# Second attention layer of a four-layer graph kernel: where the output bias and the second beta are added

## Chip, cores and metric

The kernel runs on one core of a Trainium2 chip. The metric is the device time of one execution in microseconds (us). Everything is float32. The engines are named as the profile names them: PE is the matrix engine (PEld its weight loads), DVE the vector engine, ACT the scalar engine, POOL GpSimd, SP the queue that issues plain DMAs.

## What is computed

A node table x of 50,000 rows of 128 goes through four layers; each is `x = layernorm(x + layer(x))`. Layers 0 and 1 are graph attention and graph convolution, layers 2 and 3 are edge attention over 25,000 edges sorted by target node. The change is in layer 2:

```python
q, k, v = x @ Wq + bq, x @ Wk + bk, x @ Wv + bv           # 8 heads of 16
score = einsum('ehd,ehd->eh', q[dst], k[src]) / sqrt(16) + edge_attr @ We + be
attn = softmax of score over the edges of each dst
out = segment_sum(attn * v[src], dst)
h = out @ Wo + bo + x                                      # bo: the output bias
x3 = layernorm(x + layernorm(h) * gamma + beta)            # beta: the "second beta", beta2 in the kernel
```

## The kernel before

Rows that no edge reaches are computed first, in a long phase over the whole node table. What follows is done for edges only, in slots of 128 edges. The last two phases are the edge attentions, `kind == 2` (layer 2) and `kind == 3` (layer 3), each one loop over 49 iterations L of 512 edges (`G_CH`, `CH = 512`, `SUB = 4` slots of 128).

Each phase is a software pipeline written as steps. A plan (lines 1679 to 1687 for layer 2) gives every step a place; the step of iteration L stands at `place + 138 * L` (`HOP4_LAG = 138`), and `Line.run` (line 860) sorts the steps of each engine by that number. So each engine does its steps of different iterations in a fixed order, and waits in that order: an engine whose next step isn't ready waits, and all behind it wait too. One turn of the loop does one step of each kind; the steps of late places belong to older iterations. Buffers form a ring of five (`RING = 5`), so that what is written for L reuses the buffer of L - 5.

The steps around the change, in layer 2:

- `gather` (POOL, lines 1776 to 1780, helper line 895): eight indirect DMAs, four that fetch the source rows `gs` and four that fetch the target rows `own`. It waits until the previous users of the buffers, five iterations ago, are done.
- `residual` (POOL, lines 1766 to 1774): two additions of 128x512, `xo = own + bo` and `w = own + beta2`.
- `turn_x`, `products`, `values`, `scores` (PE): `turn_x` turns `gs`, `own` and the edge attributes; `products` are the key and query products (lines 1835 and 1836), `values` the value product (1848), `scores` two accumulated products (1856 and 1858) whose result is waited for by DVE.
- `maximum` (DVE, lines 931 to 938): starts with a copy (931), then a running maximum (933) and three element-wise operations (935, 936, 938); `sums` (DVE, 953, 957, 960) makes messages and running sums `den` and `num`.
- `turn_sums` (PE): turns `num` (line 368, `ps<-ident,num`), multiplies columns for the next layer's query (1883), and turns `den` into rows (965). `divide` (DVE, 2023, 973, 975, 978) follows it.
- `turn_o` (PE) turns the divided result `o` (in the buffer `kb`), `copy_oT` (ACT, 1940) copies it out of PSUM into `xsT`, `turn_q` (PE) turns the finished rows of an older iteration (`msg`), and `rows_o` (PE, lines 1867 to 1871) multiplies by Wo: four blocks of 128 columns (helper `rows_times`, lines 371 to 378, where the product is line 374), each opening its own part of the PSUM bank K[7].
- `h_res` (DVE, lines 2034 to 2039) adds the bank K[7] and `xo`. Two layernorms (`ln_vector`, lines 319 to 332) with `x3_pre` (2043 to 2050, which reads `w`) between them follow.

Within one turn of the loop DVE's order is: scale of an older iteration (329, 332), `maximum`, `h_res`, statistics (319), `x3_pre` (2047, 2050), statistics, `sums`, scale, `qk` (2006), `divide`. PE's order is: `turn_o`, `turn_q`, `rows_o`, `turn_x`, `products`, `values`, `turn_sums`, `scores`.

An earlier phase has already a product of the kind that the change adds, in `xw_rows` (line 1303): a 1x128 row of ones times a 1x512 bias row opens a bank (line 1306), and four 128x128 blocks are accumulated on it (line 1308).

Of the kernel before, what the change touches and what calls it, by code (L numbers as in the profile page):

```python
# [15 lines left out]
F32 = mybir.dt.float32  # L16
# [3 lines left out]
ALU = mybir.AluOpType  # L20
# [3 lines left out]
P = 128  # L24
D = 128
SUB = 4
CH = P * SUB
NODES, EDGES = 50000, 25000
RING = 5
# [18 lines left out]
def build(nc, x, src, dst, ea32, ea64, ew, w, out):  # L48
# [13 lines left out]
    def S(name):  # L62
        if name not in sems:
            if len(sems) == len(handles):
                handles.append(ctx.enter_context(nc.semaphore(f"signal_{len(handles)}")))
            sems[name] = handles[len(sems)]
        return sems[name]
# [32 lines left out]
    ones = sb("ones", [1, P])  # L100
# [11 lines left out]
    Wq, Wk, Wv, Wo = (sb(n, [P, D]) for n in ("Wq", "Wk", "Wv", "Wo"))  # L112
    bq, bk, bv = (sb(n, [P, 1]) for n in ("bq", "bk", "bv"))
    bo, gamma2, beta2 = (sb(n, [P, D]) for n in ("bo", "gamma2", "beta2"))
# [16 lines left out]
    def rows4(t):  # L131

        return t.rearrange("p (j f) -> p j f", j=SUB)

    def each_row(row):
        return row[:, None, :].to_broadcast([P, SUB, D])
# [234 lines left out]
    def rows_times(pe, to, tT, W, bias_row=None):  # L371

        for j in range(SUB):
            last = nc.tensor.matmul(to[:, j * D:(j + 1) * D], tT[:, j * P:(j + 1) * P], W[:],  # L374
                                    start=True, stop=bias_row is None)
            if bias_row is not None:
                last = nc.tensor.matmul(to[:, j * D:(j + 1) * D], ones[:], bias_row[:], start=False, stop=True)
        return last
# [22 lines left out]
    with ExitStack() as tmp:  # L401
# [4 lines left out]
        xsT, xdT = ring("xsT", 2, (P, CH)), ring("xdT", 2, (P, CH))  # L406
# [574 lines left out]
    K = [ps[:, k, :] for k in range(8)]  # L981
# [9 lines left out]
    with ExitStack() as tmp:  # L991
# [9 lines left out]
        own = tile("own")  # L1001
# [672 lines left out]
    for kind in (2, 3):  # L1674
# [2 lines left out]
        table, ea = tables[kind + 1], (ea32 if kind == 2 else ea64)  # L1677
        if kind == 2:
            lag, plan = HOP4_LAG, {
                "load": (1, "ea_in pen_in"), "residual": (30, "xo x2b"),  # L1680
                "turn_x": (38, "xsT_ps xdT_ps eaT_ps"), "copy_xT": (66, "xsT xdT eaT"), "products": (84, "k_ps q_ps"),
                "values": (101, "v_ps"), "copy_z": (112, "kb"), "qk": (120, "qk"), "scores": (129, "z_ps"),
                "maximum": (149, "M_first M dz Dm0 Dm"), "gather": (-420, ""), "exps": (181, "p F"),
                "sums": (232, "msg den num"), "turn_sums": (255, "num_rows"), "divide": (270, "dn rd divided"),
                "turn_o": (285, "oT_ps"), "copy_oT": (296, "oT"), "rows_o": (304, "wo_ps"), "h_res": (317, "h_res"),
                **ln_plan("d", 326, 394, 419, 439), "x3_pre": (478, "dg x3_pre"), **ln_plan("e", 494, 510, 528, 547),
                "store": (565, "stored"), "turn_q": (574, "x3T_ps"), "copy_q": (592, "x3T")}
        else:
            lag, plan = HOP5_LAG, {
                "load": (1, "ea_in pen_in ew_in q_in own_in"),  # L1690
                "turn_x": (72, "xsT_ps eaT_ps"), "copy_xT": (100, "xsT eaT"), "residual": (105, "xo"), "products": (136, "z_ps"),
                "gather": (-420, ""), "values": (163, "v_ps"), "copy_z": (174, "kb"), "qk": (218, "zl"),
                "maximum": (227, "M_first M dz Dm0 Dm"), "exps": (261, "p F"), "sums": (286, "msg den num"),
                "turn_sums": (342, "num_rows"), "divide": (403, "dn rd divided"), "x4_pre": (416, "x4_pre"),
                **ln_plan("f", 474, 490, 516, 522), "scatter": (540, "")}
        new_phase()
        with ExitStack() as tmp:
            hop = Line(tmp, f"t{kind}", plan, lag, "xsT pen kb qk p F den num msg xo " + ("xdT w" if kind == 2 else "own u x4"),
                      {"gs": (table, NT + GT, slot_idx), **({"own": (table, NT + GT, own_idx)} if kind == 2 else {})})
            B = hop.B  # L1700
            for L, b in enumerate(B):
                b["ea"] = tmp.enter_context(nc.sbuf_tensor(f"ea_{kind}_{L}", [P, SUB * width], F32))
                b["eaT"] = tmp.enter_context(nc.sbuf_tensor(f"eaT_{kind}_{L}", [width + (1 if kind == 2 else 5), CH], F32))
                if kind == 2:

                    b["o"], b["u"], b["v"], b["xn"] = b["kb"], b["F"], b["p"], b["msg"]
                else:
                    b["o"] = b["kb"]
# [11 lines left out]
            with nc.Block() as block:  # L1720
# [41 lines left out]
                @block.gpsimd  # L1762
                def _(pool):
                    step = hop.steps()

                    if kind == 2:
                        @step("residual")
                        def _(L):

                            b = B[L % RING]  # L1770
                            step.due_dma(pool, "ea_in", L)
                            hop.due_gathered(pool, L)
                            nc.gpsimd.tensor_tensor(rows4(b["xo"][:]), rows4(b["own"][:]), each_row(bo), ALU.add).then_inc(S("xo"), 1)
                            nc.gpsimd.tensor_tensor(rows4(b["w"][:]), rows4(b["own"][:]), each_row(beta2), ALU.add).then_inc(S("x2b"), 1)

                    @step("gather")
                    def _(L):
                        for name in ["xsT_ps"] + ["xdT_ps", "xo", "x2b"] * (kind == 2):
                            step.due(pool, name, L, RING)
                        hop.gather(pool, L)  # L1780

                    if kind == 3:
                        @step("scatter")
                        def _(L):

                            step.due(pool, "f_out", L)
                            for t in range(SUB):
                                k = L * SUB + t
                                pool.indirect_dma_start(out=out, out_offset=bass.IndirectOffsetOnAxis(ap=end_idx[:, k:k + 1], axis=0),  # L1789
                                                        in_=B[L % RING]["x4"][:, t * D:(t + 1) * D], in_offset=None,  # L1790
                                                        bounds_check=NODES - 1, oob_is_err=False).then_inc(pool_dma[f"scattered{L % RING}"], 16)

                    step.run()
                    hop.end_gathers(pool)
                    if kind == 3:
                        for L in range(G_CH - RING, G_CH):
                            pool.wait_ge(pool_dma[f"scattered{L % RING}"], 16 * SUB * (L // RING + 1))

                @block.tensor
                def _(pe):  # L1800
                    step = hop.steps()
                    if kind == 2:
                        pe.wait_ge(S("be_row"), RING)
                    else:
                        for k in range(8):
                            nc.tensor.transpose(K[6 + k // 4][:, k % 4 * P:(k % 4 + 1) * P], q_all[:, k // 2, k % 2 * P:(k % 2 + 1) * P], ident[:]).then_inc(S("q_turned_ps"), 1)
                        pe.wait_ge(S("q_suf"), 1)
                        nc.tensor.transpose(K[3][0:1, 0:P], q_suf[:, 0:1], ident[:]).then_inc(S("q_suf_ps"), 1)
                        pe.wait_ge(S("q_bwd"), 1)
                        nc.tensor.transpose(K[4][0:1, 0:P], q_sum[:, 0:1], ident[:]).then_inc(S("q_first"), 1)  # L1810
                        pe.wait_ge(S("q_rows"), 1)
                        nc.tensor.transpose(K[5][:, 0:1], q_rows[:, 1:P + 1], ident[0:1, 0:1]).then_inc(S("q_last"), 1)
# [37 lines left out]
                    if kind == 2:  # L1850
# [16 lines left out]
                        @step("rows_o")  # L1867
                        def _(L):
                            step.due(pe, "oT", L)
                            step.due(pe, "h_res", L, 1)  # L1870
                            rows_times(pe, K[7], B[L % RING]["xsT"], Wo).then_inc(S("wo_ps"), 1)

                        @step("turn_q")
                        def _(L):
# [89 lines left out]
                def _(v):  # L1964
                    V = nc.vector
                    step = hop.steps()
                    if kind == 2:
                        for b in B:
                            V.memset(b["eaT"][width:width + 1, :], 1.0).then_inc(S("be_row"), 1)
                        V.memset(q_all[:], 0.0).then_inc(S("q_none"), 1)  # L1970
# [60 lines left out]
                        divide(v, step, b, L, K[4], K[5], heads, 1e-8 if kind == 2 else 1e-16, b["o"])  # L2031

                    if kind == 2:
                        @step("h_res")
                        def _(L):
                            b = B[L % RING]
                            step.due(v, "wo_ps", L)
                            step.due(v, "xo", L)
                            V.tensor_tensor(b["u"][:], K[7], b["xo"][:], ALU.add).then_inc(S("h_res"), 1)

                        ln_vector(v, step, B, "d", "u", "h_res")

# [69 lines left out]
```

## Time and profile before

| what | us |
|---|---|
| median of 3 runs | 4333.93 |
| lowest and highest | 4331.24, 4335.06 |
| profiled execution, its own time | 4329.79 |
| its span, first to last instruction | 4328.1 |
| around the span (difference) | 1.7 |

| engine | busy us | share of the span | instructions |
|---|---|---|---|
| PE | 2921.5 | 68% | 12128 |
| PEld | 1943.4 | 45% | 12128 |
| DVE | 3475.1 | 80% | 8069 |
| ACT | 2494.4 | 58% | 5486 |
| POOL | 2522.2 | 58% | 2300 |

The mean granted clock of PE is 0.74 of full speed. Layer 2's loop lies at some 2793 to 3676 us of the span, a fifth of it. The shares of the whole span are averages over eight phases with different limits, so the change has to be read from the rows of this one.

### The profile page before, as it was taken

Reading aid. Unit: us, or ns where it says so; the run is one execution under the profiler, and the core shown is the slowest. Engines: PE = TensorE matmul, PEld = TensorE weight load, DVE = VectorE, ACT = ScalarE, POOL = GpSimd, SP = SyncE. Lnnn points to the kernel's source line nnn. Section 1 sums busy time; section 2 is a strip of 40 time slices with the busy share of each in tenths; the row PEclk is TensorE's granted clock in tenths of the full one; section 3 lists DMA queues with packets and bytes.
Section 4 is the critical chain, followed back from the end, with each engine's and each line's share of the span. In section 5 each row is a group of like instructions: output and inputs, shape, how many; then the busy total and the mean of one; then the engine's idle time right before and its main releaser. Section 6 shows DMA issues by size and latency. Waiting matters only on the chain. (4 is left out here: it accounts for less than half of the span.)

```text
span 4328.1 us, 48774 instructions
## 1 busy us (share of the span) xinstructions
PE 2921.5 (68%) x12128; PEld 1943.4 (45%) x12128; DVE 3475.1 (80%) x8069; ACT 2494.4 (58%) x5486; POOL 2522.2 (58%) x2300
## 2 busy tenths in 40 slices
PE   5777767777673178874545545478888887677775
PEld 3544444454442034444545534345555554344443
DVE  5999999999998678875656679768777776788886
ACT  3777777777776256762323334446656565455554
POOL 6655555545450166626767767588666650766664
PEclk9998898888986578777767755577777776656555
DMA  4876666555553388854444456422222220333331
GB/s 114 178 186 186 185 190 187 186 190 187 187 181 132 103 246 255 252 165 124 152 128 151 152 164 198 154 62 72 66 68 64 67 62 28 106 88 87 92 95 49
DMA packets 383765, 599.12 MB, mean 138 GB/s; under 512 B 124231, under 2 KB 205296, under 8 KB 383486
## 3 DMA queue, kind: packets, MB, share of 16 engines
q1 hardware_dynamic: 313726, 482.99, 36.5%
q0 software_dynamic: 69760, 113.02, 10.5%
q8 instruction: 101, 1.65, 0.2%
q14 instruction: 178, 1.46, 0.1%
HBM read 312.45 MB, written 287.17 MB: 139 GB/s over the span
## 5 line engine op out<-in xcount | busy, mean ns | idle before, releaser
L1555 POOL DMA_INDIRECT gs_g<-table_xw,slot_idx x588 | 593.9, 1010 | 296.9 <-issue 263.7
L900 POOL DMA_INDIRECT gs_t<-table_x,slot_idx x392 | 421.5, 1075 | 300.8 <-issue 198.5
L495 POOL DMA_INDIRECT gs<-x,src_idx x200 | 224.2, 1121 | 441.1 <-DMA xd_rows<-gd 368.8
L368 PE MATMUL ps<-ident,gs_g 128*128 128x128 f32 x588 | 137.1, 377 | 363.2 <-DMA gs_g<-table_xw,slot_idx 363.2
L1593 ACT ACTIVATE hT_g<-u_g 128x512 f32<-128x512 f32 x147 | 92.5, 629 | 497.7 <-DVE u_g L1642 497.7
L1272 POOL DMA_INDIRECT slot_idx<-node_map,src_idx x200 | 242.8, 1214 | 190.9 <-DMA slot_idx<-node_map,src_idx 94.6
L1635 DVE TENSOR_TENSOR_SCAN agg_g<-same_seg,agg_g,ps 128x512 f32<-128x512 uint8 x147 | 188.0, 1279 | 173.9 <-PE ps L368 173.6
L483 POOL DMA_INDIRECT node_map<-slot_no,end_idx x200 | 278.8, 1394 | 60.9 <-issue 60.3
L1789 POOL DMA_INDIRECT out<-x_t,end_idx x196 | 205.6, 1049 | 169.6 <-ACT x_t L339 116.9
L368 PEld LDWEIGHTS ps<-ident,gs_g 128*128 128x128 f32 x588 | 90.0, 190 | 402.6 <-issue 352.0
L495 POOL DMA_INDIRECT gd<-x,dst_idx x200 | 215.4, 1077 | 60.9 <-issue 60.0
L1848 PE MATMUL ps<-xsT_t,Wv 128*128 128x512 f32 x196 | 152.3, 870 | 133.0 <-DVE msg_t L953 132.8
L900 POOL DMA_INDIRECT own_t<-table_x,own_idx x196 | 200.3, 1022 | 59.7 <-issue 59.7
L1630 DVE SCALAR_TENSOR_TENSOR own_g<-bs_row,root,own_g 128x128 f32<-128x128 f32 x588 | 167.2, 346 | 48.7 <-DMA own_g<-table_xw 48.2
L628 ACT ACTIVATE h1T<-ps,h_bias 128x512 f32<-128x512 f32 x49 | 33.7, 687 | 268.7 <-DVE nm L775 267.9
L1940 ACT COPY xsT_t<-ps 128x512 f32<-128x512 f32 x49 | 28.7, 585 | 250.3 <-PE ps L368 250.3
L596 ACT ACTIVATE x_b<-v_b,nm,rs 128x128 f32<-128x128 f32 x392 | 156.6, 497 | 19.4 <-DVE nm L775 19.4
L596 ACT ACTIVATE x_b<-s_b,nm,rs 128x128 f32<-128x128 f32 x392 | 156.8, 497 | 17.1 <-DVE nm L775 17.1
L596 ACT ACTIVATE hf_b<-hf_b,nm,rs 128x128 f32<-128x128 f32 x392 | 157.5, 514 | 2.4 <-DVE nm L775 2.4
L596 ACT ACTIVATE x_b<-t_b,nm,rs 128x128 f32<-128x128 f32 x392 | 157.4, 510 | 0.0
L374 PE MATMUL ps<-WS,hT_g 128*128 128x128 f32 x784 | 152.9, 362 | 5.5 <-ACT xw_g L1601 5.5
L1913 ACT COPY xsT_t<-ps 128x512 f32<-128x512 f32 x98 | 56.4, 576 | 171.8 <-PE ps L368 171.8
(362 smaller groups left out, 10071.3 us busy)
## 6 DMA issues: line engine op xcount, KB each, us to landing
table_xw<-xw_b SPq DMA_DIRECT2D x147, 512.0 KB, 5.4
table_x<-x_b SPq DMA_DIRECT2D x98, 512.0 KB, 2.7
own_g<-table_xw SPq DMA_DIRECT2D x147, 256.0 KB, 3.7
x_in<-x SPq DMA_DIRECT2D x49, 512.0 KB
out<-hf_b SPq DMA_DIRECT2D x49, 512.0 KB, 2.9
table_xw<-xw_g SPq DMA_DIRECT2D x98, 256.0 KB
pen_t<-pen_row SPq DMA_DIRECT2D x98, 256.0 KB, 4.1
xd_rows<-gd SPq DMA_DIRECT2D x50, 256.0 KB, 5.6
```

Of the source, the lines that this page charges most:

```text
L368: last = nc.tensor.transpose(to[0:width, j * P:(j + 1) * P], t[:, j * width:(j + 1) * width], ident[:])
L374: last = nc.tensor.matmul(to[:, j * D:(j + 1) * D], tT[:, j * P:(j + 1) * P], W[:], start=True, stop=bias_row is None)
L483: pool.indirect_dma_start(out=node_map, out_offset=bass.IndirectOffsetOnAxis(ap=end_idx[:, t:t + 1], axis=0), in_=slot_no[:, t:t + 1], in_ ...
L495: pool.indirect_dma_start(out=to[k % 3][:, j * D:(j + 1) * D], out_offset=None, in_=x, in_offset=bass.IndirectOffsetOnAxis(ap=of[:, n:n + ...
L596: last = nc.scalar.activation(to[:, k * D:(k + 1) * D], of(k), ACT.Identity, scale=r[:, n, k:k + 1], bias=b[:, n, k:k + 1])
L900: pool.indirect_dma_start(out=self.B[L % RING][g][:, t * D:(t + 1) * D], out_offset=None, in_=table, in_offset=bass.IndirectOffsetOnAxis(a ...
L1272: pool.indirect_dma_start(out=slot_idx[:, t:t + 1], out_offset=None, in_=node_map, in_offset=bass.IndirectOffsetOnAxis(ap=src_idx[:, t:t + ...
L1555: pool.indirect_dma_start(out=gs[c % 6][:, j * D:(j + 1) * D], out_offset=None, in_=tables[layer], in_offset=bass.IndirectOffsetOnAxis(ap= ...
L1630: V.scalar_tensor_tensor(out=blk, in0=bs_row[layer][:], scalar=root4[:, k:k + 1], in1=blk, op0=ALU.mult, op1=ALU.add).then_inc(S("own_bias ...
L1635: V.tensor_tensor_scan(agg[t % 3][:], same_seg[:, t * CH:(t + 1) * CH], T_X[t % 2], agg[(t - 1) % 3][:, CH - 1:CH], ALU.mult, ALU.add).the ...
L1789: pool.indirect_dma_start(out=out, out_offset=bass.IndirectOffsetOnAxis(ap=end_idx[:, k:k + 1], axis=0), in_=B[L % RING]["x4"][:, t * D:(t ...
L1848: nc.tensor.matmul(K[3], (Wv if kind == 2 else Wv3)[:], B[L % RING]["xsT"][:], start=True, stop=True).then_inc(S("v_ps"), 1)
```

## The change

In layer 2's loop alone:

- POOL's `residual` step goes. `xo` and its buffers go.
- `rows_o` now begins with one product of a 1x128 row of ones and a 1x512 row `bo_row4` (bo four times), which writes the whole bank K[7]; the four blocks of Wo are accumulated on it.
- `h_res` adds the bank and `own` itself.
- A new DVE step `residual` at place 130 makes `w = own + beta2`.
- `gather` of iteration L now waits for `h_res` of L - 5 (it waited for `xo`) since `own` is read until then, and for `w` as before.
- Once ahead of the loop, DVE fills `bo_row4` and PE waits for it.

```diff
-                "load": (1, "ea_in pen_in"), "residual": (30, "xo x2b"),
+                "load": (1, "ea_in pen_in"), "residual": (130, "x2b"),
...
+                bo_row4 = tmp.enter_context(nc.sbuf_tensor("bo_row4", [1, CH], F32))
...
-                    if kind == 2:
-                        @step("residual")
-                        def _(L):
-
-                            b = B[L % RING]
-                            step.due_dma(pool, "ea_in", L)
-                            hop.due_gathered(pool, L)
-                            nc.gpsimd.tensor_tensor(rows4(b["xo"][:]), rows4(b["own"][:]), each_row(bo), ALU.add).then_inc(S("xo"), 1)
-                            nc.gpsimd.tensor_tensor(rows4(b["w"][:]), rows4(b["own"][:]), each_row(beta2), ALU.add).then_inc(S("x2b"), 1)
-
                     @step("gather")
                     def _(L):
-                        for name in ["xsT_ps"] + ["xdT_ps", "xo", "x2b"] * (kind == 2):
+                        for name in ["xsT_ps"] + ["xdT_ps", "h_res", "x2b"] * (kind == 2):
...
                         pe.wait_ge(S("be_row"), RING)
+                        pe.wait_ge(S("bo_row4"), 1)
...
                             step.due(pe, "oT", L)
                             step.due(pe, "h_res", L, 1)
-                            rows_times(pe, K[7], B[L % RING]["xsT"], Wo).then_inc(S("wo_ps"), 1)
+                            nc.tensor.matmul(K[7], ones[:], bo_row4[:], start=True, stop=False, skip_group_check=True)
+                            for j in range(SUB):
+                                last = nc.tensor.matmul(K[7][:, j * D:(j + 1) * D], B[L % RING]["xsT"][:, j * P:(j + 1) * P], Wo[:],
+                                                        start=False, stop=j == SUB - 1, skip_group_check=True)
+                            last.then_inc(S("wo_ps"), 1)
...
+                        V.tensor_copy(bo_row4.rearrange("o (j f) -> o j f", j=SUB), bo[0:1, None, :].to_broadcast([1, SUB, D])).then_inc(S("bo_row4"), 1)
...
                     if kind == 2:
+                        @step("residual")
+                        def _(L):
+                            b = B[L % RING]
+                            hop.due_gathered(v, L)
+                            V.tensor_tensor(rows4(b["w"][:]), rows4(b["own"][:]), each_row(beta2), ALU.add).then_inc(S("x2b"), 1)
+
                         @step("h_res")
                         def _(L):
                             b = B[L % RING]
                             step.due(v, "wo_ps", L)
-                            step.due(v, "xo", L)
-                            V.tensor_tensor(b["u"][:], K[7], b["xo"][:], ALU.add).then_inc(S("h_res"), 1)
+                            V.tensor_tensor(b["u"][:], K[7], b["own"][:], ALU.add).then_inc(S("h_res"), 1)
```

## Rows read from the trace of the kernel before

**Rows 1.** Busy time in layer 2's loop: PE, PEld, DVE, ACT, POOL; clock; DMA.
```profile
2846.00:3620.00 774.00, 653.23 (x2613) 423.70 (x2612) 597.46 (x1084) 473.18 (x906) 501.05 (x449) 0.74 0.24 65
```

**Rows 2.** DVE's waits, 2844 to 3640: line, releaser, total, times, longest.
```profile
DVE q_all L2023 <- PE ps L965: 79.5, 45, 3.4
DVE M_t L931 <- PE ps L1858: 77.8, 46, 2.4
DVE F_t L2039 <- PE ps L374: 10.0, 20, 0.8
```

**Rows 3.** PE in order of time, one turn: start, duration, idle before.
```profile
3223.08 2.07 PE L1858 MATMUL ps<-qk_t,head_sum 128*128 128x512 f32 x2
3226.73 1.08 PE L368 MATMUL ps<-ident,msg_t 128*128 128x128 f32 x4 [0.72 <-issue]
3227.61 1.91 PE L374 MATMUL ps<-Wo,xsT_t 128*128 128x128 f32 x8
3229.32 1.06 PE L368 MATMUL ps<-ident,gs_t 128*128 128x128 f32 x4
```

**Rows 4.** DVE in order of time, the same turn.
```profile
3221.19 0.17 DVE L2023 COPY q_all<-ps 128x16 f32<-128x16 f32 x1 [1.71 <-PE ps L965]
3225.19 0.15 DVE L931 COPY M_t<-M_t 128x1 f32<-128x1 f32 x1 [2.34 <-PE ps L1858]
3227.30 1.16 DVE L936 TENSOR_TENSOR F_t<-pen_t,M_t 128x512 f32<-128x512 f32 x1
3229.56 0.69 DVE L2039 TENSOR_TENSOR F_t<-ps,xo_t 128x512 f32<-128x512 f32 x1 [0.37 <-PE ps L374]
```

**Rows 5.** PE, then DVE, in order of time, a turn with the faster clock at `rows_o`.
```profile
3245.35 1.06 PE L374 MATMUL ps<-Wo,xsT_t 128*128 128x128 f32 x8
...
3243.34 0.15 DVE L931 COPY M_t<-M_t 128x1 f32<-128x1 f32 x1 [2.34 <-PE ps L1858]
3246.78 0.68 DVE L2039 TENSOR_TENSOR F_t<-ps,xo_t 128x512 f32<-128x512 f32 x1
```

**Rows 6.** Busy time, products with Wo alone: PE, PEld, clock, DMA share, GB/s.
```profile
2844.00:3640.00 796.00, 82.39 (x376) 78.20 (x376) 0.74 0.24 63
```

**Rows 7.** PE in order of time, the one-row product in the earlier phase.
```profile
1569.06 2.04 PE L1306 MATMUL ps<-bias_row,ones 1*128 1x512 f32 x2 [0.24 <-ACT xw_b_h L1347]
1571.03 2.08 PE L1308 MATMUL ps<-WI,x1T_h 128*128 128x128 f32 x8
1572.90 1.06 PE L368 MATMUL ps<-ident,x_b_h 128*128 128x128 f32 x4
...
1577.93 1.12 PE L1306 MATMUL ps<-bias_row,ones 1*128 1x512 f32 x2
1578.98 1.16 PE L1308 MATMUL ps<-WI,x1T_h 128*128 128x128 f32 x8
```

**Rows 8.** DVE by line, 2844 to 3640: count, busy, mean ns.
```profile
L936 DVE TENSOR_TENSOR F_t<-pen_t,M_t 128x512 f32<-128x512 f32 x47 | 50.5, 1074 | 0.0
L938 DVE TENSOR_TENSOR F_t<-F_t,M_t 128x512 f32<-128x512 f32 x47 | 41.3, 878 | 1.6
```

**Rows 9.** The same by line in layer 3's loop, 3720 to 4300.
```profile
L938 DVE TENSOR_TENSOR F_t<-F_t,M_t 128x512 f32<-128x512 f32 x47 | 32.5, 692 | 1.6
L936 DVE TENSOR_TENSOR F_t<-pen_t,M_t 128x512 f32<-128x512 f32 x47 | 32.2, 684 | 0.0
L2059 DVE TENSOR_TENSOR xo_t<-own_t,bias 128x512 f32<-128x512 f32 x46 | 31.4, 684 | 0.0
```

**Rows 10.** POOL in order of time, one turn.
```profile
3226.64 1.28 POOL L1774 TENSOR_TENSOR w_t<-own_t,beta 128x512 f32<-128x512 f32 x1
```

**Rows 11.** The page's group of the gathers of `own`.
```profile
L900 POOL DMA_INDIRECT own_t<-table_x,own_idx x196 | 200.3, 1022 | 59.7 <-issue 59.7
```

**Rows 12.** DVE in order of time, first iterations.
```profile
2827.58 0.69 DVE L938 TENSOR_TENSOR F_t<-F_t,M_t 128x512 f32<-128x512 f32 x1
2835.01 0.69 DVE L2039 TENSOR_TENSOR F_t<-ps,xo_t 128x512 f32<-128x512 f32 x1 [6.74 <-POOL xo_t L1773]
```

More of the change, by code:

```diff
@@ L1697, in build @@
         with ExitStack() as tmp:
-            hop = Line(tmp, f"t{kind}", plan, lag, "xsT pen kb qk p F den num msg xo " + ("xdT w" if kind == 2 else "own u x4"),
+            hop = Line(tmp, f"t{kind}", plan, lag, "xsT pen kb qk p F den num msg " + ("xdT w" if kind == 2 else "xo own u x4"),
                       {"gs": (table, NT + GT, slot_idx), **({"own": (table, NT + GT, own_idx)} if kind == 2 else {})})
             B = hop.B
+            if kind == 2:
+                bo_row4 = tmp.enter_context(nc.sbuf_tensor("bo_row4", [1, CH], F32))
             for L, b in enumerate(B):
```

## Prediction

> **What bounds the kernel now.** The change touches one phase, so I read the busy times of its stretch first and not those of the page. In the 774 us of layer 2's steady loop PE is busy 653 us (84%), DVE 597 us (77%), ACT 473 and POOL 501, at a mean granted clock of 0.74 [rows 1]. No engine is full. That is what a ring of waits looks like, and the list of DVE's waits says where the ring runs: DVE waits for PE before line 2023 (79.5 us in 45 waits, 1.77 each), before line 931 (77.8 us in 46, 1.69 each) and, little, before `h_res` (10.0 us in 20) [rows 2]. In order of time one turn is then: `scores` end on PE, DVE starts `maximum` at 3225.19 while PE goes on to `turn_o`, `turn_q` and the product with Wo; the two meet at `h_res`, at 3229.56, where DVE had waited 0.37 us for the product [rows 3, 4]; DVE runs on to the end of `num`; PE turns `num` and does the `scores` of the next iteration while DVE does some short steps and then waits; and round again. So three legs follow on each other: from line 931 to `h_res`, on which DVE and PE run side by side and the later one counts; DVE alone; PE alone. 376 records of the product with Wo at 8 a turn are 47 turns in 796 us [rows 6], 16.9 us each.
>
> **First leg, how the two stand.** PE's side: from 931 to `h_res` 3229.56 - 3225.19 = 4.37 us, with the product with Wo starting 2.42 us after 931 and taking 1.91 [rows 3, 4]. That is with the slow clock, 1.2 GHz. In a turn with the clock at 2.4 GHz the product starts 2.01 us after 931 and takes 1.06, so PE is ready at some 3.1 us, and `h_res` starts after 3246.78 - 3243.34 = 3.44 us, on DVE's account alone [rows 5]. Which clock is usual there: the product takes 82.39 us / 47 = 1.75 us a turn [rows 6], which is 0.82 of turns at 1.91 and 0.18 at 1.06. DVE's side: 3.44 us undisturbed. Line 936 takes 1074 ns here and 684 in layer 3's loop, line 938 takes 878 and 692 [rows 8, 9]; the excess of 0.39 + 0.19 = 0.58 us falls where POOL's additions run (line 1774 from 3226.64 for 1.28 us lies over 936, which took 1.16) [rows 4, 10]. The leg's mean is thus 3.44 + 0.58 + 10.0 / 47 of waiting = 4.23 us.
>
> **The change part by part.**
>
> 1. *The one-row product in `rows_o`.* The same product stands in an earlier phase. From its start to that of the next it took 1571.03 - 1569.06 = 1.97 us with the slow clock and 1578.98 - 1577.93 = 1.05 with the fast one; one row costs what 128 rows cost (2.07 for `scores`' product, 2.04 for this) [rows 3, 7]. Blocks that follow such a product took 1572.90 - 1571.03 = 1.87 us, those of Wo here, after a turn, 3229.32 - 3227.61 = 1.71 [rows 3, 7]: 0.16 more. It stands behind the wait for `oT` and behind `turn_q`, which waits for the same copy, so PE's idle 0.72 us before `turn_q` [rows 3] don't take it up. All of it lies between `turn_o` and `h_res`: PE's side becomes 4.37 + 1.97 + 0.16 = 6.50 us with the slow clock and 3.1 + 1.05 + 0.16 = 4.3 with the fast one. Both are later than DVE. With the shares of before the leg is 0.82 x 6.50 + 0.18 x 4.3 = 6.10 us, 1.87 more than 4.23. The ends for this cost: 0.1 a turn (all fast) and 2.27 (all slow). I keep the measured share, since what PE does before this place, `scores` and `turn_o`, is unchanged.
>
> 2. *POOL's additions go.* DVE's side of the first leg loses 0.58 us. By itself that would bring next to nothing, since PE's side is at 4.37 in most turns and DVE waits there already; with part 1 it is fully behind PE. Worth 0 a turn; up to 0.58 if the product weren't added.
>
> The Trainium skill (SBUF — State Buffer, section "SBUF: two separate sides") says that a GpSimd instruction and a DVE instruction with two SBUF inputs lock each other out for a whole instruction. The trace agrees for 936 and 938. By that rule alone the change would save 48 x 0.58 = 28 us; the sum goes by the order of the legs instead.
>
> 3. *`w` on DVE.* The same addition takes 684 ns on DVE in layer 3's loop [rows 9]. Its place 130 puts it between `qk` (120) and `divide` (270 - 138 = 132), just where DVE idles 1.77 us on average [rows 2], 1.71 in the turn shown [rows 4]. That idle time hides it: 0. If the cover went, it would cost 48 x 0.68 = 33 us. POOL's gathers run beside it; line 2059 and its gathers run together in layer 3 and it stays at 684. Its wait for the gathers was met by PE in `turn_x`, before.
>
> 4. *`gather` waits for `h_res` of L - 5.* In places: h_res stands at 317 - 5 x 138 = -373, the rows are wanted at 38, so 411 places, or 411 / 138 = 3.0 turns of 17 us, are left for eight gathers of 1.02 + 0.30 us, 10.6 us, and their landing [rows 11]. Nothing is queued behind the waiting POOL but later gathers. 0. SP's queue isn't touched.
>
> 5. *Start of the phase.* The first `h_res` waits 6.74 us for `xo`, which POOL makes only after four iterations' gathers [rows 12]. That wait goes. What is late next: DVE is ready at 2827.58 + 0.69 = 2828.3 [rows 12], and the product, which now has 1.05 to 1.97 us more before it, can take back at most that. I take 6.7 us, once, and 4.7 as its lower end. Filling `bo_row4` is one short DVE instruction while all wait for the first gathers: 0.
>
> **Sum.** 48 turns x 1.87 = 90 us, less 6.7 = +83 us. Against the profiled execution: 4328.1 + 1.7 + 83 = 4413. The median of the runs is 4.1 us above that execution, so I predict 4417.
>
> **The rivals.**
>
> *The clock is at 2.4 GHz more often.* Since the loop's turns get longer and PE busier, the level at `rows_o` may fall otherwise. If half the turns are fast there, the leg is 5.40 us, +1.17 a turn, +56 - 7 = +49: 4383. For it: the clock changes within every turn, and its mean is 0.74 [rows 1]. Against it: the share of 0.82 slow turns.
>
> *Faster: PE stays at 2.4 GHz through `scores` and `rows_o`.* Then the first leg is 4.3 us, as now, the one-row product is free, and `scores`, whose two products take 2 x 1.97 us slow and 2 x 1.05 fast, come up to 1.8 us sooner in each slow turn; with half of that gained in 48 turns and the 6.7 us: 0.9 x 48 + 7 = 50 us less, 4284. It decides once at most one turn in twenty is slow at `rows_o` and those two products gain. Against it: `turn_o` still waits for DVE and PE still idles before it and before `turn_q`.
>
> The Trainium skill (TensorE: Matmul & The Clock Gate, Part 1, "What's actually happening") says that a busy PE is granted the full clock and that idle stretches take it away. By that rule more work on PE speaks for this rival; no row here shows whether a product of one row counts as work, and the trace's slow turns follow 84% busy time.
>
> *Dearer: PE is late for `num` too.* The slow clock lasts until the key, query and value products, which then end after `num`, and the leg of DVE alone is lengthened. Five products' worth at 0.9 us more each, less the idle time PE has before `num`: some 1.2 us a turn, 48 x 3.1 - 7 = +142: 4476. The point from which it decides: `values` ends later than DVE's `num`.
>
> *It doesn't matter.* DVE's side, not PE's, sets the leg, and the product hides under the 0.58 us of stretch and the waits elsewhere. Against it: the 0.37 and 0.72 us of waits show no room for 2 us.
>
> **How the numbers follow.** Forecast (4390 to 4450): 0.67. Clock half fast (4365 to 4390): 0.13. Dearer (4450 to 4490): 0.10. Faster by the clock: 0.06. No change: 0.04. The range takes the first two and the near part of the third: 4372 to 4462. A measurement of this kernel tells about 0.2% from no change. Chances: faster 0.06, within 0.2% 0.03, slower 0.91.
>
> **What would show it.** In the profile after: one-row products at line 1871's place x98 records, some 2 us before the blocks of Wo; `h_res` waiting for PE in nearly all 49 turns, some 2.5 us each; 936 at 684 and 938 at 692 ns; the new addition at 684 with the idle time before 2023 down from 1.77 to about 1.1; no wait of POOL's that reaches `turn_x`; the first `h_res` near 2828. The prediction is wrong if the clock's share at Wo moves from 0.82 slow, if `num` is turned late, or if the addition of `w` moves line 2023.

## The result and the profile after

The changed kernel takes 4376.36 us (median of 6 runs, 4363.36 to 4385.35) against 4336.68 for the kernel before beside it (6 runs, 4331.24 to 4343.18). The ratio is 1.0087, 95% interval 1.0066 to 1.0108: by it 38 us slower (the medians lie 40 us apart). Two more measurements of the same pair, further down, give 32 and 34 us in the medians. I had forecast 83 us, 4417. The direction is right and the size is less than half; the time lies just inside my range of 4372 to 4462, at its low end, and 4417 is above all six runs.

The profiled execution took 4381.33 us with a span of 4379.6. Of its 51.5 us over that of before, 43.6 lie in layer 2's loop: from the first memset of the phase on DVE to `q_turned` it took 3729.5 - 2799.7 = 929.8 us against 3676.8 - 2790.6 = 886.2. The other 8 us are a phase that began 9.1 us later and an end 1.2 us shorter, in code that is the same in both. The two profiled executions lie 12 us further apart than the medians do, so what follows accounts for this pair.

Busy time by stretch, layer 2's loop after: PE, PEld, DVE, ACT, POOL, clock, DMA (of before: [rows 1]).

```profile
2846.00:3680.00 834.00, 730.82 (x2743) 435.48 (x2744) 597.06 (x1148) 490.46 (x919) 407.50 (x357) 0.74 0.23 61
```

PE is now busy 88% of the stretch, POOL 49% in the place of 65%; the mean clock is the same 0.74. DVE's waits, 2844 to 3690 (of before: [rows 2]):

```profile
DVE F_t L2042 <- PE ps L1866: 114.7, 46, 3.1
DVE M_t L931 <- PE ps L1851: 70.5, 47, 2.3
DVE q_all L2021 <- PE ps L965: 40.9, 45, 1.2
```

`h_res` waits for PE in 46 of 47 turns, 2.5 us each: the product lies on the path, as forecast. The wait before line 2021 fell from 1.77 to 0.91 us, more than the 0.68 us of the addition that now stands there. Two turns of after in order of time, the first with the slow clock between `turn_o` and `h_res`, the second with the fast one; PE first:

```profile
3242.89 1.30 PE L1851 MATMUL ps<-qk_t,head_sum 128*128 128x512 f32 x2
3243.99 1.06 PE L368 MATMUL ps<-ident,kb_t 128*128 128x128 f32 x4
3245.77 1.09 PE L368 MATMUL ps<-ident,msg_t 128*128 128x128 f32 x4 [0.72 <-issue]
3246.79 2.07 PE L1864 MATMUL ps<-bo_row,ones 1*128 1x512 f32 x2
3248.79 2.08 PE L1866 MATMUL ps<-Wo,xsT_t 128*128 128x128 f32 x8
3250.66 1.06 PE L368 MATMUL ps<-ident,gs_t 128*128 128x128 f32 x4
...
3230.65 1.12 PE L1864 MATMUL ps<-bo_row,ones 1*128 1x512 f32 x2
3231.70 1.16 PE L1866 MATMUL ps<-Wo,xsT_t 128*128 128x128 f32 x8
```

and DVE in the same two turns:

```profile
3244.23 0.15 DVE L931 COPY M_t<-M_t 128x1 f32<-128x1 f32 x1 [0.62 <-PE ps L1851]
3250.90 0.69 DVE L2042 TENSOR_TENSOR F_t<-ps,own_t 128x512 f32<-128x512 f32 x1 [3.15 <-PE ps L1866]
...
3228.55 0.15 DVE L931 COPY M_t<-M_t 128x1 f32<-128x1 f32 x1 [1.31 <-PE ps L1851]
3232.89 0.69 DVE L2042 TENSOR_TENSOR F_t<-ps,own_t 128x512 f32<-128x512 f32 x1 [0.82 <-PE ps L1866]
```

The first leg is 6.67 us slow and 4.34 fast (forecast 6.50 and 4.3; before 4.37 and 3.44 [rows 4, 5]). DVE by line, 2844 to 3690:

```profile
L938 DVE TENSOR_TENSOR F_t<-F_t,M_t 128x512 f32<-128x512 f32 x47 | 32.5, 692 | 1.6
L936 DVE TENSOR_TENSOR F_t<-pen_t,M_t 128x512 f32<-128x512 f32 x47 | 32.0, 681 | 0.0
L2036 DVE TENSOR_TENSOR w_t<-own_t,beta 128x512 f32<-128x512 f32 x46 | 31.3, 681 | 0.0
```

The stretches of 936 and 938 [rows 8] are gone with POOL's additions, and the new addition costs what the row of layer 3 said [rows 9].

**The turn leg by leg.** To see the whole turn I took four legs from the times of every turn in the trace: from the start of line 931 to `h_res`; on to the end of `num` (line 960); on to the start of `scores` (the product with `we_rep`); on to the next 931. Means of 44 turns, from the fourth on, in us, with the share of turns whose clock is slow ahead of `h_res` (its level between 1.0 and 0.5 us before it):

| kernel | 931 to `h_res` | to `num` | to `scores` | to 931 | turn | slow share |
|---|---|---|---|---|---|---|
| before | 4.27 | 6.71 | 2.64 | 3.50 | 17.12 | 0.80 |
| after | 5.98 | 6.62 | 2.34 | 3.28 | 18.22 | 0.70 |
| difference | +1.71 | -0.09 | -0.30 | -0.22 | +1.10 | |

The first leg took nearly what was forecast (1.87). The forecast left the other three as they were, and they gave back 0.61.

The leg to `scores` has two parts: how late PE starts to turn `num` once DVE has it, and the small products that follow. After the change PE is never late (0.06 us in each of the 44 turns), and the leg is 2.33 to 2.60 us whichever the clock at `h_res`. Before, PE was 0.5 to 1.3 us late in 5 of the 44 turns, which makes 0.12 of the 0.30 us; the other 0.18 are small products that ran slow in some turns.

### The profile page after: what moved, and what is told of

It is laid out like the page before. It is cut to its first block and busy times, and to the rows that moved or that the text cites. A ratio compares the mean times of both kernels' runs of the same rounds, so it can differ in the third digit from the quotient of the medians.

```text
span 4379.6 us, 48825 instructions
## 1 busy us (share of the span) xinstructions
PE 2987.2 (68%) x12226; PEld 1951.0 (45%) x12226; DVE 3470.1 (79%) x8119; ACT 2505.4 (57%) x5486; POOL 2436.6 (56%) x2202
## 5 line engine op out<-in xcount | busy, mean ns | idle before, releaser
L900 POOL DMA_INDIRECT gs_t<-table_x,slot_idx x392 | 447.8, 1142 | 512.2 <-PE ps L368 269.6
L483 POOL DMA_INDIRECT node_map<-slot_no,end_idx x200 | 291.4, 1457 | 61.0 <-issue 60.7
```

Source lines behind the costliest of these rows:

```text
L483: pool.indirect_dma_start(out=node_map, out_offset=bass.IndirectOffsetOnAxis(ap=end_idx[:, t:t + 1], axis=0), in_=slot_no[:, t:t + 1], in_ ...
L900: pool.indirect_dma_start(out=self.B[L % RING][g][:, t * D:(t + 1) * D], out_offset=None, in_=table, in_offset=bass.IndirectOffsetOnAxis(a ...
```

## Experiments

Each kernel is the changed one with one edit, shown in short form, and its ratio is to the kernel before on the same chip. The groups ran on different chips; on the one of e1 to e4 the kernel before takes 4597.87 us, since phases other than this one are longer there, so the times of those four are not set beside those of other groups.

### Without the product; both additions on DVE; the product elsewhere; 128 rows (e1 to e4)

```diff
 e1_no_row
-  matmul(K[7], ones, bo_row4, start=True, stop=False); 4 x matmul(K[7][j], xsT[j], Wo, start=False)
+  rows_times(pe, K[7], b["xsT"], Wo)
 e2_both_on_dve: e1, and in DVE's residual
+  V.tensor_tensor(rows4(b["xo"]), rows4(b["own"]), each_row(bo), ALU.add)      # h_res adds xo again
 e3_row_in_gap: the opening product as a step of its own
+  "open_o": (245, "")                   # between values and turn_sums
 e4_rows_128: the opening product over 128 rows
-  matmul(K[7], ones[1 x 128],  bo_row4[1 x 512], ...)
+  matmul(K[7], ones[128 x 128], bo_row4[128 x 512] (bo / 128 in each row), ...)
```

> The changed kernel without the one-row product (bo is left out of the result); the additions stay moved. Theory (the product is the whole cost, and some of it comes back because the clock's levels fall elsewhere in the turn): the leg from line 931 to h_res falls back from 5.98 us to about 4.2 (PE's side 4.37 slow, DVE's 3.44), a turn to about 17.0, and the time to some 10 us below the kernel before, near 4325, the gain of the phase's start. Rival (the moved additions or the later gathers cost too): the time stays above the kernel before.

> Both additions, xo and w, on DVE at place 130, no one-row product; PE's work is that of the kernel before. Theory: two times 0.68 us fit in the 1.77 us that DVE idles before line 2021, so the turn is that of e1_no_row within 0.2 us and the time near 4325 to 4335. Rival: DVE's idle time is really needed (the clock is fast when the den rows are made, and the idle time is short then), so the turn grows by up to 0.68 us, 33 us in all, to about 4360.

> The one-row product as a step of its own between values and turn_sums, where PE waits about 1 us for num; the rest as changed. Theory (it costs by its place): it runs there at the fast clock in 1.05 us and is hidden, the leg to h_res is back at 4.2 us plus at most 0.16, and the time is near 4330. Rival (PE's total work sets the turn through the clock): it still costs, and the time stays near 4376.

> The product that opens the bank is made with 128 rows (all ones, times bo / 128 in each row) in the place of one; the same 512 columns, same place. Theory 1 (a one-row product counts for the clock as any other): nothing changes, 4376 and a share of slow clock at h_res of 0.70. Theory 2 (a one-row product keeps the clock down): the levels fall otherwise, the slow share at h_res drops clearly below 0.70, and the time falls by more than 10 us.

Measured: e1 0.9940 (0.9919 to 0.9960), e2 0.9999 (0.9978 to 1.0021), e3 1.0008 (0.9986 to 1.0031), e4 1.0068 (1.0043 to 1.0093). Without the product the kernel is faster than before, so the product is all that costs. The rest was less clean. e2 had a shorter turn in its trace than e1 (16.56 us against 16.78) and yet the longer time. e3 was 31 us slower than e1, where I expected some 5. e4 had a shorter first leg (5.24 us) and a turn of 18.23; its slow share stayed at 0.68, so nothing in it speaks for theory 2, that one row keeps the clock down. All were therefore run again beside the others on chips like the first.

### The change once more, w on POOL, the product twice (c1, c2, e5, e6)

```diff
 e5_w_on_pool
-  "residual": (130, "x2b")   on DVE
+  "residual": (30, "x2b")    on POOL
 e6_row_twice
+  matmul(K[7], ones, bo_row4, start=True, stop=False)      # a second time
```

> The kernel before, unchanged, for a trace on the chip of this group. The additions of POOL lie over lines 936 and 938, the turn is near 17.1 us and h_res comes 4.3 us after line 931, as in the first trace; if the earlier phases take longer on another chip, layer 2's loop still shows the same legs.

> The changed kernel again, on the chip of this group: a turn of 18.2 us, the leg from line 931 to h_res of 6.67 us at 1.2 GHz and 4.34 at 2.4, and a time 35 to 55 us above the kernel before. Rival (the first measurement's 40 us were that chip's): clearly less or more than that.

> The changed kernel with w made on POOL again at its old place; the one-row product and the longer hold of own stay. Theory (the addition is hidden on DVE, and DVE's side of the first leg is covered by PE's): the time is that of c2_after within 10 us, though line 936 or 938 is stretched again. Rival (the addition costs on DVE): up to 33 us faster than c2_after.

> The product that opens the bank is made twice, one after the other. Theory (each lies whole between turn_o and h_res): the leg at 1.2 GHz grows from 6.67 to 8.7 us, at 2.4 GHz from 4.34 to 5.4; by levels alone that is 1.7 us a turn, 82 us; if the same share is given back by the legs behind it as in the changed kernel (a third), about 50 us above c2_after. Rival (PE's extra work raises the share of 2.4 GHz until it pays): less than 25 us above c2_after.

Measured: c2 1.0075 (1.0061 to 1.0089), 4368.72 us; e5 1.0083 (1.0060 to 1.0107), 4372.47; e6 1.0304 (1.0282 to 1.0326), 4465.93. The change costs 32 us here, a little below the 35 to 55 expected. c1 is one execution, 4330.90 us. The legs, as above:

| kernel | 931 to `h_res` | to `num` | to `scores` | to 931 | turn | slow share |
|---|---|---|---|---|---|---|
| c1_before | 4.43 | 6.72 | 2.61 | 3.40 | 17.17 | 0.66 |
| c2_after | 6.04 | 6.62 | 2.34 | 3.23 | 18.22 | 0.73 |
| e5_w_on_pool | 6.09 | 6.64 | 2.33 | 3.24 | 18.30 | 0.75 |
| e6_row_twice | 7.70 | 6.62 | 2.51 | 3.30 | 20.14 | 0.98 |

The change repeats leg by leg. The slow share of the kernel before does not: 0.80 in one execution, 0.66 in another, with the same turn within 0.05 us. So its fall from 0.80 to 0.70 in the first pair doesn't repeat either: here it rose, from 0.66 to 0.73. Where `w` is made doesn't matter while the product is there: 3.7 us between e5 and c2, inside both intervals, though one addition on POOL stretches line 936 again, to 920 ns. DVE by line in e5, 2860 to 3640:

```profile
L936 DVE TENSOR_TENSOR F_t<-pen_t,M_t 128x512 f32<-128x512 f32 x42 | 38.6, 920 | 0.0
L938 DVE TENSOR_TENSOR F_t<-F_t,M_t 128x512 f32<-128x512 f32 x43 | 31.0, 721 | 1.5
```

A second product costs 97 us, twice the 50 that I expected of it. PE in e6, a slow turn:

```profile
3232.32 2.07 PE L1864 MATMUL ps<-bo_row,ones 1*128 1x512 f32 x2
3234.19 1.91 PE L1865 MATMUL ps<-bo_row,ones 1*128 1x512 f32 x2
3236.03 2.08 PE L1867 MATMUL ps<-Wo,xsT_t 128*128 128x128 f32 x8
```

Its slow leg grew to 8.37 us, and here nothing came back: nearly every turn is slow at `h_res` (0.98), and the turn grew by 1.92. So the give-back is no fixed share; the theory of "a third" fell.

### The four versions again (e7 to e10)

The new one puts the product where PE idles while ACT copies `o`:

```diff
 e10_row_before_oT
+  "open_o": (286, "")                   # between turn_o and turn_q
```

> As e1_no_row (no one-row product, bo left out of the result), to be read on a second chip. Theory (the product is all that the change costs): 15 to 30 us below the kernel before, as it was 0.6% below there; a turn of 16.8 us. Rival (e1's gain was that chip's): within 5 us of the kernel before.

> As e2_both_on_dve, on a second chip. Theory (1.37 us of additions fit in DVE's idle time of 1.77 us, POOL's stretches go): the time is that of e7_no_row within 8 us, so below the kernel before, a version that beats both. Rival (the additions fill the idle time that is short when the clock is fast): 15 to 30 us above e7_no_row, so at the kernel before.

> As e3_row_in_gap, on a second chip. In its first trace the leg from line 931 to h_res was 4.11 us, but the share of slow clock there was 0.73 against 0.41 in e1_no_row, and a turn 17.40 against 16.78. Theory (the product is hidden where it stands, but the clock takes half of the gain back): 15 to 30 us above e7_no_row, at the kernel before within 10 us. Rival: as e7_no_row.

> The one-row product as a step between turn_o and turn_q, where PE idles 0.72 us while ACT copies; the rest as changed. Theory (it costs by its place on the path to h_res): the slow leg falls from 6.67 to about 5.95 us, a turn by 0.4 to 0.7 us, and the time by 20 to 35 us against the changed kernel, to some 5 to 15 us above the kernel before. Rival (a turn is set by PE's work through the clock, not by the place): within 10 us of the changed kernel.

| kernel | ratio, interval | us | 931 to `h_res` | to `scores` | to 931 | turn | slow share |
|---|---|---|---|---|---|---|---|
| before | 1 | 4334.46 | | | | | |
| e7_no_row | 0.9914, 0.9899 to 0.9928 | 4299.13 | 3.88 | 3.15 | 3.37 | 17.02 | 0.48 |
| e8_both_on_dve | 0.9928, 0.9913 to 0.9942 | 4303.26 | 3.86 | 3.05 | 3.27 | 16.79 | 0.45 |
| e9_row_in_gap | 1.0006, 0.9992 to 1.0021 | 4337.57 | 4.22 | 2.86 | 3.74 | 17.44 | 0.84 |
| e10_row_before_oT | 0.9957, 0.9944 to 0.9970 | 4316.65 | 4.46 | 2.91 | 3.05 | 17.04 | 0.43 |

(The leg to `num` is 6.62 in all four.) Three things follow. First, moving the additions alone is worth 35 us (e7; 37 by the ratio), more than the 15 to 30 expected and not the 6.7 us of the phase's start. Its trace explains only a part: it is of the slowest of e7's seven runs (4317.64 us, 17 below the kernel before), with a turn 0.10 to 0.15 us shorter and a start some 10 us shorter. The first leg is 0.39 to 0.55 us shorter there, but the leg to `scores` takes most of it back: in all 23 turns whose clock is fast at `h_res`, the key, query and value products run slow in part and PE turns `num` 0.9 to 1.3 us late.

Second, the product in its place costs 1.0075 - 0.9914, 1.6% or 70 us, against the 90 forecast. Third, e8 computes everything and is 31 us faster than the kernel before. DVE's two additions and the wait behind them in e8:

```profile
3263.29 0.68 DVE L2032 TENSOR_TENSOR w_t<-own_t,beta 128x512 f32<-128x512 f32 x1
3263.89 0.68 DVE L2033 TENSOR_TENSOR xo_t<-own_t,bo 128x512 f32<-128x512 f32 x1
3266.08 0.17 DVE L2017 COPY q_all<-ps 128x16 f32<-128x16 f32 x1 [1.51 <-PE ps L965]
```

In this turn both fit and 1.5 us of idle time are left.

e9's product was hidden where I put it in 37 of the 44 turns; PE, one of them:

```profile
3321.50 1.02 PE L1841 MATMUL ps<-xsT_t,Wv 128*128 128x512 f32 x2
3322.45 1.12 PE L1856 MATMUL ps<-bo_row,ones 1*128 1x512 f32 x2
3323.73 0.66 PE L368 MATMUL ps<-ident,num_t 128*128 128x128 f32 x4 [0.16 <-DVE num_t L960]
3326.00 1.70 PE L1849 MATMUL ps<-eaT,we_rep 33*128 33x512 f32 x2
```

It took 1.12 us at the fast clock out of an idle time that still has 0.16 left. In the other 7 turns the products before it run slow and PE comes to it late; PE, then DVE's `num`, in one of them:

```profile
2987.33 1.60 PE L1841 MATMUL ps<-xsT_t,Wv 128*128 128x512 f32 x2
2988.86 1.12 PE L1856 MATMUL ps<-bo_row,ones 1*128 1x512 f32 x2
2989.92 0.66 PE L368 MATMUL ps<-ident,num_t 128*128 128x128 f32 x4
...
2986.20 1.26 DVE L960 TENSOR_TENSOR_SCAN num_t<-F_t,num_t,msg_t 128x512 f32<-128x512 f32 x1
```

`num` is there at 2987.46 and is turned from 2989.92, 2.46 us later. In these 7 turns the leg to `scores` takes 4.7 to 5.1 us; no turn of e7 has more than 3.54. By its median e9 is 38 us slower than e7. The traces show half of that, 48 x 0.42 = 20 us, as e7's is of its slowest run. Of the 0.42 us a turn, the product's own 1.1 us in 7 of 44 turns is 0.18. The rest comes with the levels of the clock: the slow share at `h_res` is 0.84 in the place of 0.48, and the leg to 931 takes 3.74 us in the place of 3.37. So a product that is hidden in most turns still cost 38 us, of which the traces put some part to the clock. My expectation of 15 to 30 had the sign and too small a size. The step in e10 lies on the path but half in PE's idle time:

```profile
3222.18 1.06 PE L368 MATMUL ps<-ident,kb_t 128*128 128x128 f32 x4
3223.17 2.07 PE L1856 MATMUL ps<-bo_row,ones 1*128 1x512 f32 x2
3225.17 1.11 PE L368 MATMUL ps<-ident,msg_t 128*128 128x128 f32 x4
3226.08 1.91 PE L1869 MATMUL ps<-Wo,xsT_t 128*128 128x128 f32 x8
```

Its slow leg is 5.61 us (6.67 in the change), its slow share 0.43, and it beats the kernel before by 18 us, where I expected 5 to 15 above it. Against e7, which has no such product, the same product costs 70 us, 38 us or 18 us by its place.

### What the product itself costs (e11 to e14)

```diff
 e13_rows_128_before_oT: e10 with the 128-row product of e4
```

> As e4_rows_128: the opening product with 128 rows. Theory 1 (the slow leg is 6.07 us in the place of 6.67, since PE doesn't idle at the change of row counts, and that reaches the time): 15 to 25 us faster than e12_after. Theory 2 (what the leg gains, the clock's levels take back in the other legs, as a turn of 18.23 us in e4 suggests): within 10 us of e12_after.

> The changed kernel once more, as the reference of this group: 32 to 40 us above the kernel before.

> The 128-row product between turn_o and turn_q, where PE idles while ACT copies. Theory 1: the slow leg falls from e10's 5.61 to about 5.2 us and the time to 25 to 30 us below the kernel before. Theory 2 (the clock takes it back): as e10_row_before_oT, 18 us below the kernel before, within 8 us.

> As e8_both_on_dve, for this group: 25 to 35 us below the kernel before, and so 60 to 70 us below e12_after. It would be the version that beats both kernels; the rival is e13_rows_128_before_oT, if its product is fully hidden.

| kernel | ratio, interval | us | 931 to `h_res` | to `scores` | to 931 | turn | slow share |
|---|---|---|---|---|---|---|---|
| e11_rows_128 | 1.0085, 1.0071 to 1.0098 | 4370.10 | 5.29 | 2.98 | 3.38 | 18.26 | 0.68 |
| e12_after | 1.0083, 1.0067 to 1.0099 | 4370.58 | 5.93 | 2.33 | 3.26 | 18.15 | 0.68 |
| e13_rows_128_before_oT | 0.9936, 0.9917 to 0.9954 | 4311.89 | 3.73 | 2.67 | 3.78 | 16.80 | 0.00 |
| e14_both_on_dve | 0.9903, 0.9889 to 0.9918 | 4295.32 | 3.90 | 2.88 | 3.25 | 16.65 | 0.50 |

e11 against e12 is the clearest pair of the study. PE in e11, one turn:

```profile
3244.82 1.03 PE L368 MATMUL ps<-ident,num_t 128*128 128x128 f32 x4 [1.24 <-DVE num_t L960]
3245.65 1.71 PE L1881 MATMUL ps<-q_cols,xdT_t 128*128 128x4 f32 x8
3247.21 1.85 PE L965 MATMUL ps<-sel,den_t 128*128 128x8 f32 x8
...
3255.53 1.91 PE L1865 MATMUL ps<-bo_row,all_ones 128*128 128x512 f32 x2
3257.24 1.71 PE L1867 MATMUL ps<-Wo,xsT_t 128*128 128x128 f32 x8
3258.78 0.60 PE L368 MATMUL ps<-ident,gs_t 128*128 128x128 f32 x4
```

With 128 rows the product takes 3257.24 - 3255.53 = 1.71 us at the slow clock, not the 2.00 of the one-row product, and starts 0.88 us after `turn_q` and not 1.02; the blocks of Wo behind it lose their 0.16. The first leg is 0.64 us shorter. The turn is not: turning the sums takes 0.65 us more, since the slow clock now comes up in some turns over lines 1881 and 965 (4.1 to 4.3 us to `scores` in such turns, 2.33 in the others). All 0.64 us came back as cost, and the two times are the same within 0.5 us. Theory 2 held. In e13 the place and the levels work together: no turn is slow at `h_res`, and it is 25 us below the kernel before; its interval and that of e10 overlap, so which of the two is faster is open.

e14 repeats e8: 42 us below the kernel before and 75 below e12. Both additions on DVE and no product on PE is the complete kernel with the lowest median, 0.72% and 0.97% faster than the kernel before in two groups. On the first chip the same kernel (e2) showed no gain, 0.9999 (0.9978 to 1.0021); why is open. e13 is 17 us slower than e14 in the median, with intervals that just touch.

## Why the prediction was wrong in size

By its own steps:

- **The ring and its three legs: right.** `h_res` waits for PE in 46 of 47 turns after [rows 2], and e7, e10 and e6 move the first leg by the place and number of the products.
- **Part 1, the product: right in both levels, too high in the mean.** 6.67 and 4.34 us against 6.50 and 4.3. The step that failed is "I keep the measured share", with the other legs left as they are. Of the 1.87 us a turn that I forecast, 1.71 came in the first leg, and the other three gave back 0.61; in the second pair (c1, c2) it is 1.61 and 0.54. So the larger miss is the legs that I put at nothing, above all the one to `scores` (0.30 and 0.27 us) and the one to 931 (0.22 and 0.17). The share was no constant either: 0.80 and 0.66 in two executions of the unchanged kernel, so my reason for keeping it, that PE's work before this place is unchanged, didn't hold. In the kernel before, every turn has some time at the slow clock, and 0.18 of the time of the leg to `scores` is slow; after, with a longer first leg, 0.01. One reading is that a longer first leg takes up slow time which the small products of `turn_sums` (2.33 us to `scores`, the shortest there is) would have had. That is argued and not shown, and e6 doesn't fit it: with a first leg that is longer still, slow time was back in the leg to `scores` (2.51 us). Why the levels fall as they do was not settled.
- **"One row costs what 128 rows cost": wrong.** The row I compared it with, that of `scores` [rows 3], stands behind a product of 33 rows. Between 128-row neighbours the 128-row product takes 1.71 us (e11) and the one-row product 2.00, with 0.14 before it and 0.16 behind: 0.6 us a slow turn. The one-row price itself was taken from the right row [rows 7], so this didn't spoil the sum.

  The Trainium skill (TensorE: Matmul & The Clock Gate, "Why this matters for your kernels") says that a single product of 32 rows takes the same time as one of 128. For a product of one row between 128-row neighbours the trace doesn't agree: 2.00 against 1.71 us.
- **Part 2, POOL's additions: worth 0 only beside the product.** e5 shows that: 3.7 us. I wrote that they would bring next to nothing by themselves, as PE was at 4.37 us anyway; e7 is 35 us faster than the kernel before with the same work on PE. Its first leg is 3.88 in the place of 4.27 to 4.43, and the clock is fast there in half of the turns. How much of the 35 us comes from that leg is not shown, since the trace explains only a part. The leg to `num` was shorter by 0.09, which I hadn't in the sum.

  The Trainium skill (SBUF — State Buffer, "SBUF: two separate sides") has GpSimd and a DVE instruction with two SBUF inputs lock each other out; 936 at 1074, 920 and 681 ns with two, one and no additions on POOL agrees. I had put the 28 us of that stretch aside for the order of the legs. For the additions alone the measured gain, 35 us with some 10 of them the start, is nearer to it than to nothing; but e7's trace has a turn only 0.10 to 0.15 us shorter, so the agreement of the sizes may be chance.
- **Part 3, `w` on DVE: right.** It is hidden; even two additions are (e8, e14).
- **Part 4, the later gathers: right.** No wait of DVE's in the list goes back to them, and e7 holds `own` as long and is the faster.
- **Part 5, the start: right, a little small.** The third iteration's line 931 comes 45.7 us after the phase's first memset and 55.6 before: 9.9 us, where I had 6.7 (c2 against c1: 11.6).

The sum corrected: 83, less 48 x (1.87 - 1.71) = 8, less 48 x 0.09 = 4, less 48 x 0.30 = 14, less 48 x 0.22 = 11, less 3 for the start, is 43 us; the phase took 43.6 us more in the profiled pair. In the second pair the turn grew by 1.05 us: 48 x 1.05 less 11.6 is 39 us, and the two executions lie 38 us apart. The time landed where my rival with half fast turns had it (4383), but not by its mechanism: the share of slow turns was still 0.70 and 0.73, and the gain came in other legs. The dearer rival, PE late for `num`, didn't come: after the change PE is late in no turn, though it is in 5 of 44 before and in 23 of e7. The faster rival, that more work on PE keeps its clock up, fell: the mean clock stayed at 0.74, and e6, with yet more work on PE, has a clock of 0.71 in the loop and nearly all turns slow at `h_res`.

What stays open is what sets the levels of the clock. e9 and e7, which differ by one product alone, have 0.84 and 0.48 of their turns slow at `h_res`; e13 shows that the same work can run with none.

## What to carry to other kernels

Where a chain goes round over two engines and one of them changes its speed within the turn, price a new step for every leg and not only for the one in which it stands: here the other three legs gave back a third of what the first had gained, with a second product nothing came back, and what the 128-row product saved in one leg was lost again in another. Before work is moved from an idle-looking engine onto the path, look for a place beside it: the same product cost 70 us in front of its consumer and 18 us in an idle slot of 0.72 us a little earlier. A slot has to be there in every turn, at either clock: e9's was gone in 7 of 44. And split a change that does two things: here one half was worth 35 us and the other cost 70, and a third way of doing the first half (both additions in DVE's idle time) beats both kernels in two groups of three. And before a difference of medians is explained by a trace, see which run the trace is of: e7's was 18 us above its median.

## What the runs showed of the hardware that I had not expected

- A one-row float32 product of 512 columns between 128-row products takes longer than one of 128 rows: 2.00 against 1.71 us at 1.2 GHz. The product before it hands over 0.14 us later, and the blocks behind it take 0.16 us longer.
- PE's granted clock can take back the whole gain of a shorter leg (e11: -0.64 in one, +0.65 in another). With a product that is hidden in 37 of 44 turns the slow share at `h_res` was 0.84, and 0.48 without it (e9, e7).
- A turn with the fast clock at `h_res` can be paid for later in the same turn: in 23 of e7's 44 turns PE then ran slow over the key, query and value products and turned `num` 0.9 to 1.3 us late.
- Two executions of the same kernel, with turns of 17.12 and 17.17 us, had 0.80 and 0.66 of their turns slow at `h_res`: such a share from one trace is no constant to build a sum on.
